# The blur's matrix products in fp32 in place of three fp16 products each

## The reference

```python
x = x + window_attention(_gn(x))     # 32 images, 192 channels, 56 x 56; windows of 7 x 7, 12 heads of 16
x = x + blur(_gn(x), offset)

# blur: every group of 24 channels is shifted by a whole number of pixels (zeros come in)
# and then convolved with a 5 x 5 Gaussian whose centre is off by the rest of the offset
disp = _displace(x.reshape(B, P, cpp, h, w), off_int).reshape(B, C, h, w)
kernel = jnp.exp(-jnp.sum(d * d, axis=-1) / (2.0 * SIGMA ** 2))
kernel = kernel / jnp.sum(kernel, axis=(1, 2), keepdims=True)
out = lax.conv_general_dilated(disp, kw, window_strides=(1, 1), padding=[(c, c), (c, c)],
                               feature_group_count=C, ...)
```

## Time and profile before

| | |
|---|---|
| median of 3 runs | 7009.8 us (7008.25 to 7031.7) |
| span of the profiled execution (first to last instruction) | 7029.0 us |
| busy, share of the span | PE 82%, PE's weight loads 55%, DVE 75%, ACT 66%, POOL 45% |
| mean granted clock of PE | 0.867 of 2.4 GHz |
| DMA | 750.73 MB, mean 107 GB/s |

### The profile page before, as it was taken

The page is one execution under the profiler, slowest core; times in us unless marked ns, Lnnn a source line. Parts: engine busy times, 40 slices in busy tenths (PEclk is TensorE's granted clock), DMA queues, the critical chain, the costliest instruction groups (busy, mean ns, idle before and its releaser), DMA issues.

```text
span 7029.0 us, 228954 instructions
## 1 busy us (share of the span) xinstructions
PE 5767.8 (82%) x79428; PEld 3835.3 (55%) x79428; DVE 5250.9 (75%) x11722; ACT 4661.4 (66%) x15619; POOL 3194.3 (45%) x3428
## 2 busy tenths in 40 slices
PE   6888878888888887788888788877888888888886
PEld 4555555555555555555555555555555555555554
DVE  4777777777778777778777787777787777777774
ACT  3766666666667666667766677666676666766673
POOL 1354444444445544445543455444455444444444
PEclk9888788888889898889878899888899888988886
DMA  3445555455555455554455554555545555545554
GB/s 79 103 98 108 106 115 116 94 108 109 114 113 112 102 108 108 113 119 98 110 110 105 114 113 101 108 111 113 116 99 111 109 108 115 115 95 108 109 105 73
DMA packets 1368963, 750.73 MB, mean 107 GB/s; under 512 B 1182938, under 2 KB 1256666, under 8 KB 1363546
## 3 DMA queue, kind: packets, MB, share of 16 engines
q1 hardware_dynamic: 1367770, 735.06, 50.8%
HBM read 156.66 MB, written 154.14 MB: 44 GB/s over the span
## 4 chain that ended last, share of the span: by engine, by line
PE 31%; DVE 17%; SPq 17%; issue 12%; POOL 8%; ACT 6%; DMA 5%; DVEq 1%; POOLq 0%; ACTq 0%
DMA xt<-in_x 5%; SPq L384 4%; SPq L390 4%; PE pTr L569 4%; PE pS L557 3%; ACT prob L773 3%; SPq L454 3%; PE pS L550 3%; POOL probn L1190 3%; PE pO L587 3%; DVE mix L941 2%; SPq L421 2%; DVE den L979 2%; PE pM L476 2%; DVE pT L988 2%
## 5 line engine op out<-in xcount | busy, mean ns | idle before, releaser
L1190 POOL TENSOR_TENSOR probn<-prob,den 128x588 f32<-128x588 f32 x1024 | 1199.4, 1171 | 2825.4 <-DVE den L984 2631.1
L773 ACT ACTIVATE prob<-pS,mx 128x49 f32<-128x49 f32 x4096 | 1177.4, 303 | 642.9 <-DVE mx L964 633.4
L587 PE MATMUL pO<-pT,vv 98*32 98x49 f16 x36864 | 773.8, 213 | 904.5 <-DVE pT L988 685.4
L988 DVE SCALAR_TENSOR_TENSOR pT<-pTr,pT 98x588 f16<-98x588 f32 x1024 | 748.6, 731 | 685.8 <-DMA xt<-in_x 381.9
L587 PEld LDWEIGHTS pO<-pT,vv 98*32 98x32 f16 x36864 | 663.6, 138 | 1047.7 <-DVE pT L988 647.4
L569 PE MATMUL pTr<-cst,probn 128*98 128x128 f32 x6144 | 1007.8, 308 | 0.0
L786 ACT ACTIVATE pT<-pTr 98x588 f16<-98x588 f32 x1024 | 682.9, 667 | 252.9 <-PE pTr L569 251.9
L773 ACT ACTIVATION_READ_ACCUMULATOR prob<-pS,mx 128x1 f32 x4096 | 848.2, 207 | 0.0
L550 PE MATMUL pS<-biasT,addb 128*128 128x196 f16 (+1 forms) x2048 | 661.4, 323 | 211.3 <-ACT prob L773 176.7
L569 PEld LDWEIGHTS pTr<-cst,probn 128*98 128x98 f32 x6144 | 729.3, 142 | 28.8 <-issue 0.3
L557 PE MATMUL pS<-kst,qst 96*64 96x98 f16 x12288 | 726.9, 227 | 0.0
(11 more groups left out here) (186 smaller groups left out, 15187.8 us busy)
## 6 DMA issues: line engine op xcount, KB each, us to landing
kst<-qks SPq DMA_DIRECT2D x1536, 98.0 KB
qst<-qks SPq DMA_DIRECT2D x1536, 49.0 KB, 1.9
kst<-mix SPq DMA_DIRECT2D x768, 98.0 KB
vv<-cv SPq DMA_DIRECT2D x1024, 73.5 KB
out<-xr SPq DMA_DIRECT2D x256, 294.0 KB
xr<-x_scratch SPq DMA_DIRECT2D x64, 882.0 KB
x_scratch<-xm SPq DMA_DIRECT2D x128, 392.0 KB, 3.0
xm<-in_x SPq DMA_DIRECT2D x32, 1176.0 KB, 15.5
```

What stands on the lines that cost most here:

```text
L587: mm = pe.matmul(pO[r:r + 32, p % 2, hp // 4, NT * win:NT * win + NT], vv[:, g % 2, win, p % PPR, a, hp::NHP], pT[0:98, p % 2, b, 2 * hp + ...
L773: a = act.activation(prob[:, p % 2, t], pS[:, 0, t], ACT.Exp, bias=mx[:, p % 2, h:h + 1], scale=-1.0, accum_out=den[:, p % 2, h:h + 1])
L988: dve.scalar_tensor_tensor(out=pT[0:98, p % 2, 1], in0=turned(), scalar=PSC, in1=pT[0:98, p % 2, 0], op0=ALU.mult, op1=ALU.subtract).then_ ...
L1190: pool.tensor_tensor(heads(probn[:, p % 2, :]), heads(prob[:, p % 2, :]), spread(den[:, p % 2, :], NT), ALU.mult).then_inc(S["norm_p"], 1)
```

## The change

Both stages take their operands in fp32. `xc` and its two instructions per block (ACT's cast, POOL's subtraction) go, and `xcf` itself is the operand of stage 0. `z` is one fp32 tensor, written by ACT alone; DVE's low part goes. `amat` is one fp32 tensor without the scale of 64, and the set-up loses two DVE instructions. `three` is replaced by one `matmul` per strip. Since stage 0 reads `xcf`, POOL's multiply into that buffer now waits for stage 0 of the block that used it two blocks earlier; the wait that ACT's cast had for this goes with the cast. Line numbers after the change are lower by 1 to 24.

```diff
-        xc = sb("xc", [SY, 2, 2, BC * HW], F16)
-        z = sb("z", [SY, 2, 2, 3 * SY], F16)
-        amat = sb("amat", [SY, 2, 2 * POS, SY], F16)
+        z = sb("z", [SY, 2, 3 * SY], F32)
+        amat = sb("amat", [SY, 2 * POS, SY], F32)
...
             def blur(i, b, stage):
                 if stage == 0:
-                    pe.wait_ge(S["xcl_p"], nth("xcl_p", i, b + 1))
+                    pe.wait_ge(S["xcf_p"], nth("xcf_p", i, b + 1))
...
-                    src = xc
+                    src = xcf[0:SY]
                 else:
-                    pe.wait_ge(S["z_dve"], nth("z_dve", i, b + 1))
+                    pe.wait_ge(S["z_act"], nth("z_act", i, b + 1))
                     src = z
...
-                    mm = three(pM[0:SY, k], src[:, b % 2, 0, k], src[:, b % 2, 1, k],
-                               amat[:, 0, m, :], amat[:, 1, m, :])
+                    mm = pe.matmul(pM[0:SY, k], src[:, b % 2, k], amat[:, m, :], start=True, stop=True,
+                                   skip_group_check=True)
...
-                        act.activation(z[:, b % 2, 0, :], pM[0:SY, 0:3 * SY], ACT.Copy,
-                                       scale=1.0 / ASC).then_inc(S["z_act"], 1)
+                        act.activation(z[:, b % 2, :], pM[0:SY, 0:3 * SY], ACT.Copy).then_inc(S["z_act"], 1)
...
-                    b = blur_step(p, 10, prev)
-                    if b is not None:
-
-                        act.wait_ge(S["xcf_p"], nth("xcf_p", i - 1, b + 1))
-                        if b >= 2:
-                            act.wait_ge(S["c1_pe"], nth("c1_pe", i - 1, b - 1))
-                        act.copy(xc[:, b % 2, 0, :], xcf[0:SY, b % 2, :]).then_inc(S["xch_a"], 1)
...
-                        dve.scalar_tensor_tensor(out=y, in0=pM[0:SY, 0:3 * SY], scalar=1.0 / ASC, in1=y,
-                                                 op0=ALU.mult, op1=ALU.add).then_inc(S["y_dve"], 1)
+                        dve.tensor_tensor(y, pM[0:SY, 0:3 * SY], y, ALU.add).then_inc(S["y_dve"], 1)
...
-                    b = blur_step(p, 12, prev)
-                    if b is not None:
-                        dve.wait_ge(S["z_act"], nth("z_act", i - 1, b + 1))
-                        dve.scalar_tensor_tensor(out=z[:, b % 2, 1, :], in0=pM[0:SY, 0:3 * SY], scalar=1.0 / ASC,
-                                                 in1=z[:, b % 2, 0, :], op0=ALU.mult,
-                                                 op1=ALU.subtract).then_inc(S["z_dve"], 1)
...
-                    b = blur_step(p, 11, prev)
-                    if b is not None:
-
-                        pool.wait_ge(S["xch_a"], nth("xch_a", i - 1, b + 1))
-                        pool.tensor_tensor(xc[:, b % 2, 1, :], xcf[0:SY, b % 2, :], xc[:, b % 2, 0, :],
-                                           ALU.subtract).then_inc(S["xcl_p"], 1)
-                        pool.wait_ge(S["xcl_p"], nth("xcl_p", i - 1, b + 1))
                     b = blur_step(p, 10, prev)
                     if b is not None:
...
+                        if b >= 2:
+                            pool.wait_ge(S["c1_pe"], nth("c1_pe", i - 1, b - 1))
```

19 lines of the change are left out of this document (8 added, 11 removed).

## The result

| | before | after |
|---|---|---|
| median, same chip, 4 runs each | 7014.3 us (7008.3 to 7031.7) | 7095.2 us (7080.5 to 7105.7) |
| span of the profiled execution | 7029.0 us | 7089.6 us |

The changed kernel is slower: ratio 1.011, 95% interval 1.0087 to 1.0133. Forecast were 7090 us and a range of 7025 to 7150. Two executions further down were far longer than the rest (13378 us of the kernel before, 7486 us of growth_only), and no ratio counts them.

The account below looks back on a forecast made before the run. PE was taken to bound most blur steps. Its growth less a little relief gave +2.54 us per image, times 31 +79, last image +2: span 7029.0 to 7110, on the median 7090 us, range 7025 to 7150.

Parts of the forecast that it names:

- The sum's main term: PE in the blur: six fp32 records of 0.0975 us per stage replace nine fp16, growth 0.16 us per stage at full clock.
- steps 15 to 19: Five blur steps bound by PE: three grow 0.32 us each, two waiting for ACT 0.16 each, together +1.28.
- The rivals with another price of a record, 0.052 or 0.155: PE's fp32 records: 0.155 us if loads stay open, about 7290 us, chance 0.07; 0.052 was the estimate's lower end.
- the one with the clock: PE's granted clock falls in the blur steps with the changed instruction mix: about 7180 us, chance 0.05.
- the new wait: POOL's multiply into xcf waits for stage 0 of the block two earlier; idle time covers it, cost 0.
- The rule weighed: PE's weight loads set the pace: 0.28 us gained per stage by estimate; as rival about 6890 us, chance 0.03.
- 13: then DVE's row decides: -0.42: Blur step 13: PE idles 0.62 us, 0.5 of it for z; then DVE's row decides, -0.42 us.
- Step 20: DVE decides: -0.42: Blur step 20: 1.13 us idle, half before scores, half before the next attend; DVE decides, -0.42 us.
- Step 24: Blur step 24: idle takes stage 0 in, DVE's 0.30 us goes, stage 1 gives 0.16 back: -0.14 us.
- Step 14: Blur step 14: 0.31 us of idle time takes stage 0 in, stage 1 adds +0.16 us.
- step 22: Middle of blur steps 21 to 23, forecast as 0.32 + 0.16 + 0.32 us: +0.16 for this step.
- The steps without a blur I take as unchanged: Steps outside 12 to 27: a later blur shifts them as a whole, their waits start from own steps; no change.

Follow-up runs that it names:

- growth_only: Changed kernel with ACT's cast, POOL's subtraction and DVE's low part of z put back, old waits, writing into unread tiles: 7117.1 us, 1.0125 of before.
- relief_only: Changed kernel's waits and lighter engines, but nine fp16 matmuls per stage as before, low parts of data being zeros: 6994.0 us, 0.996 of before.
- four_xcf: Changed kernel with four xcf buffers instead of two, so POOL's multiply waits for stage 0 four blocks back: 7100.0 us, 1.01 of before.
- one_fp16_product: relief_only with one fp16 matmul per strip instead of three, products with low parts left out: 6918.1 us, 0.9857 of before.
- z_fp32_six_blocks: Kernel before with stage 1 in fp32 and no low part of z in blocks 0, 1, 8, 9, 12, 13: 7050.5 us, 1.0055 of before.
- fp32_steps_12_19: The change in blocks 0 to 7 alone, the other eight as in the kernel before: 7028.4 us, 1.0022 of before.
- stage1_fp32: Kernel before with stage 1 alone in fp32, DVE's low part of z dropped: 7054.4 us, 1.006 of before.
- fp32_steps_20_27: The change in blocks 8 to 15 alone, the other eight as in the kernel before: 7028.5 us, 1.0023 of before.
- before_fewer_copies: Kernel before without the second copy of K's high part, 30 issues per group instead of 36: 6880.0 us, 0.9808 of before.
- before_copies_on_act: Kernel before with the six repeated K copies per group started by ACT instead of SP, nothing left out: 6933.5 us, 0.989 of before.
- stage0_fp32: Kernel before with stage 0 alone in fp32, ACT's cast and POOL's subtraction dropped: 7073.7 us, 1.0074 of before.
- after_fewer_copies: Changed kernel without the second copy of K's high part, 30 issues per group instead of 36: 6971.4 us, 0.9925 of before.

## Why the prediction came out right, and where it didn't

**The sum's main term held.** Two records per fp32 matmul, 0.098 us apart (0.0975 taken). The growth of a step with both stages is 0.34 us in steps 15, 19, 23 and 27 (0.32 taken), of one with an open wait of ACT 0.13 and 0.17 in steps 16 and 18 (0.16 taken); steps 15 to 19 +1.33 us (+1.28). At half clock, in the last image, the records stand 0.187 apart, and its fifteen gaps from `y` to `y` grew from 58.8 to 61.9 us, +3.1 (+2 taken). The rivals with another price of a record, 0.052 or 0.155, and the one with the clock are out. That the other engines' relief is worth less than the growth is shown by relief_only, -0.4%, and that the new wait costs nothing that can be measured by four_xcf. POOL's idle time before the scaling fell from 23.1 us in sixteen steps to 13.1, 0.6 per step and not the 1.1 taken.

**The rule weighed.** The Trainium skill (TensorE: Matmul & The Clock Gate, section LDWEIGHTS) gives a load the time of its columns divided by 1.2 per ns, which is, as an estimate, 93 ns for 112. For fp16 the trace contradicts it as a pace, 0.052 us. The fp32 records' 0.098 lies close to it. Whether the load or the stream sets the fp32 pace no run here tells, since none changed one alone.

**"13: then DVE's row decides: -0.42" had the size and not the cause.** The step fell by 0.49, but growth_only, which keeps that work, falls by 0.45. Steps 12 and 13 hold together: the pair gave back 0.14 us net in the change, against a forecast of +0.06.

**"Step 20: DVE decides: -0.42" was twice too much.** It gave 0.23, in relief_only too, and 5.77 or 5.78 us is its length in all seven kernels that drop the low part of `z` there, one_fp16_product aside. That DVE decides was right: PE still waits for its `pT` before the next attend, 0.41 us in relief_only and 0.24 after the change (0.56 before). What was wrong is that all of the 0.42 reaches `pT`. On DVE in step 20, before and after:

```profile
2386.07 0.51 DVE L1090 BATCH_NORM_STATS2 gst<-xm 128x6 f32 x1
2386.50 0.74 DVE L988 SCALAR_TENSOR_TENSOR pT<-pTr,pT 98x588 f16<-98x588 f32 x1
```

```profile
2395.18 0.55 DVE L1071 BATCH_NORM_STATS2 gst<-xm 128x6 f32 x1
2395.76 0.77 DVE L976 SCALAR_TENSOR_TENSOR pT<-pTr,pT 98x588 f16<-98x588 f32 x1
```

From the start of the step's attend the statistics begin at 4.78 us before and 4.37 after, `pT` at 5.21 and 4.95 (means of 29 images): 0.15 of it is lost between these two, and why was not found. Step 24 shows the other bound: of 0.42 it gives 0.25 back in relief_only (4.95 us) and 0.19 after the change (5.01), and in both PE has almost no idle time left (0.08 and 0.01 us, 0.46 before). There the relief of a late engine ends at the second latest, PE.

**Idle time was counted as taking in more than it did.** Step 14 grew by 0.34 and not 0.16, step 22 by 0.47 and not 0.16. In step 14 PE waits for DVE's `cv` behind stage 0, 0.26 us before and 0.27 after, so the growth took nothing of it up; in step 22 it waits 0.26 us for `cv` after and 0.13 for ACT before. The start of DVE's row in step 14, where attend begins at 2346.25 before and at 2354.09 after:

```profile
2346.20 0.51 DVE L1049 SCALAR_TENSOR_TENSOR xr<-pM,xr 112x336 f32<-112x336 f32 x1
```

```profile
2354.20 0.51 DVE L1037 TENSOR_TENSOR xr<-pM,xr 112x336 f32<-112x336 f32 x1 [0.86 <-PE pM L619]
```

Relieved of `z`, DVE now waits at `y` for PE's longer stage 1, so its row starts 0.15 us later against attend than before, `cv` in it 0.16 later (means of 29 images), and moves along with PE. These two steps and step 20 account for 0.68 of the 0.70 us by which +3.24 exceeds +2.54; the rest are small differences of both signs.

**"The steps without a blur I take as unchanged" was the step that failed.** They gave 1.06 us per image back (0.58 in steps 28 to 31, 0.48 in steps 0 to 11), so that 2.19 us times 31 = 68 us stayed where 79 had been forecast. The blur steps alone would have made 100 us, so the forecast came out near by two errors that nearly cancel, which is luck. The reason given was that the waits of these steps, the reading of the next image among them, start from steps of their own. SP's issues don't: its row begins in step 25 and goes on at its own pace, and the reading of the next image stands in such a row too, behind the copies of step 7. The table is worked out from the traces, in us. Its first two columns count from the start of step 25. Then come PE's idle time in step 31 for the last copies and before the attend with which the next step begins, and a pause of DVE that is told below. The first three columns and the pause are means of 28 images, the others of 29:

| kernel | last copy of K issued | step 31 begins | difference | idle for copies | idle before attend | DVE's pause | step 31 lasts |
|---|---|---|---|---|---|---|---|
| before | 35.24 | 33.81 | +1.43 | 0.72 | 4.36 | 4.43 | 9.95 |
| z_fp32_six_blocks | 35.31 | 34.22 | +1.09 | 0.50 | 3.85 | 4.09 | 9.21 |
| relief_only | 35.35 | 34.33 | +1.02 | 0.71 | 3.92 | 4.06 | 9.76 |
| one_fp16_product | 34.29 | 33.67 | +0.62 | 0.21 | 4.06 | 4.17 | 9.10 |
| fp32_steps_12_19 | 34.38 | 33.78 | +0.60 | 0.41 | 3.78 | 4.08 | 9.01 |
| stage1_fp32 | 35.19 | 34.64 | +0.55 | 0.44 | 3.75 | 3.96 | 9.03 |
| fp32_steps_20_27 | 35.08 | 34.66 | +0.42 | 0.24 | 3.83 | 3.97 | 8.90 |
| after | 35.04 | 35.32 | -0.28 | 0.16 | 3.82 | 3.79 | 8.80 |
| growth_only | 35.00 | 35.30 | -0.30 | 0.25 | 3.71 | 3.77 | 8.80 |
| before_fewer_copies | 32.98 | 33.51 | -0.53 | 0.00 | 4.10 | 3.83 | 8.88 |
| four_xcf | 34.94 | 35.65 | -0.71 | 0.04 | 3.72 | 3.60 | 8.54 |
| before_copies_on_act | 33.05 | 33.80 | -0.75 | 0.01 | 4.06 | 3.78 | 8.85 |
| stage0_fp32 | 34.92 | 35.67 | -0.75 | 0.14 | 3.46 | 3.48 | 8.39 |
| after_fewer_copies | 33.15 | 35.14 | -1.99 | 0.00 | 3.42 | 3.32 | 8.20 |

Growth on PE in steps 25 to 30 moves step 31 later, and SP's row stays where it is: in the change 1.5 us more for PE, 0.2 less for SP. As the difference falls step 31 gets shorter. PE is busy in it 4.87 us before and 4.82 after; the 1.15 us are idle time, 0.56 of it for the last copies (0.72 to 0.16) and 0.54 before the next attend (4.36 to 3.82). Around that attend the loop of each engine's program goes round. DVE stops 4.0 us into the step, ahead of the `pT` that attend needs, waiting for nothing that the profile shows; before the change:

```profile
2452.62 0.77 DVE L988 SCALAR_TENSOR_TENSOR pT<-pTr,pT 98x588 f16<-98x588 f32 x1 [4.47 <-issue]
2453.97 0.77 PE L587 MATMUL pO<-pT,vv 98*32 98x49 f16 x36 [3.66 <-DVE pT L988]
```

The pause comes in the 29 images whose step 31 ends a round of the loop. The last image in the loop has none, and its step 31 lasts 5.27 us before and 4.85 after. Across the runs the pause tends to be shorter the earlier SP is through with the copies; why was not tested.

So the time that came back in step 31 has two parts. For the wait for copies the cause is shown: it is gone with fewer copies, and with the same copies started by ACT. The shorter pause goes along with it and its cause is open. In fp32_steps_20_27 it is PE's growth too that closes the gap between SP and PE; in fp32_steps_12_19 it is SP, which is through 0.86 us sooner.

**Why the whole costs more than its halves.** Step 31 gives each of them about the same, 1.15 us against 0.94 and 1.05, so the whole gets it once and not twice. And step 29 takes something: 6.13 us in the changed kernel, 5.75 before, 5.55 and 5.52 in the halves, in all of them behind 1.0 us of idle time for DVE's `pT` at the end of step 28. Its mean granted clock is 0.72 after, 0.72 in growth_only and 0.67 in four_xcf, against 0.86 before and 0.86 and 0.85 in the halves; the step ahead of it is at 0.98 to 1.00 in all of them. PE's idle time in step 29 fell (0.46 us before, 0.06 after) while its busy time grew from 5.29 to 6.07 us with the same matmuls, so the lower clock goes with the longer step; what makes it fall there was not tested.

**Open.** The 0.48 us of steps 0 to 11, a difference of two means that are each uncertain by 0.4: it is gone in growth_only (93.73 us), which has the changed kernel's growth, and +0.76 instead in the pair with fewer copies. Step 5 alone differs by 0.49 and step 7 by 0.55 the other way. fp32_steps_12_19 has no fp32 work behind step 19, and yet its twelve copies of K from `qks` are issued in 7.6 us in place of 8.7 (the mean of before); why SP's pace changes was not found. Also open is step 0 of z_fp32_six_blocks. The profiled spans differ by 61 us and the medians by 81; the spans lie 15 us above the one median and 6 below the other, within the spread of the runs. What is said by steps holds for this pair of executions: 68 us in 31 images and 3 in the last make 71, and the 10 us less lie outside the 29 images of the means.

## What to carry to other kernels

Price a change of number format on TensorE by records, not by multiplications: at 112 columns one fp32 matmul costs two records of 0.098 us, each nearly twice an fp16 one of 0.052, so three fp16 products were cheaper than one fp32 product. Relief on the other engines is worth something only in the steps where they are late, and there only down to the second latest (step 24). Before taking the steps behind the change as unchanged, look at the engine that issues the DMAs: a row of issues without gaps takes up growth, and holds up whatever is issued behind it, the next image's rows here. Moving a few of the issues to another engine was worth as much (1.1%) as the whole change cost. When adding up the idle time of a step, count the wait that ends with the next step's first instruction: most of step 31's was there.
